# Start of a LoRA and mixture-of-experts kernel: fillers from a constant, raw LoRA products on partition quarters, x in two loads, GpSimd reordered

## The chip, the cores and the metric

The kernel runs on one core of a Trainium2 chip. The metric is the device time of one execution in microseconds (us); lower is better. A core has five engines with a program of their own each: TensorE (PE in the profile; its weight loads are PEld), VectorE (DVE), ScalarE (ACT), GpSimd (POOL) and SyncE (SP), which here only issues DMAs. They wait for each other on semaphores.

## The reference

Input `x` is `[2, 1024, 256]`. Each of its two sequences goes through a ReLU feed-forward layer with LoRA corrections (a common one and one of eight experts, chosen by an input number), and the result through a mixture of experts: a router takes the mean over the tokens, a softmax and the top two of eight experts; their gelu layers are added with the router's weights. `x` is added at the end.

```python
# L0_cond, x: [2, 1024, 256], F = 1024, rank 16 + 16, ALPHA = 2
hidden_i = x @ wi.T + ALPHA * (x @ common_wi_a.T) @ common_wi_b.T + ALPHA * (x @ Wa[e].T) @ Wb[e].T
hidden_i = relu(hidden_i)
hidden_o = hidden_i @ wo.T + (the same two corrections with the wo factors)
# L0_ffn
probs = softmax(hidden_o.mean(axis=1) @ gate_w)
top_w, top_i = top_k(probs, 2);  top_w /= top_w.sum()
out = sum over the two experts e of top_w * (gelu(hidden_o @ w1[e] + b1[e]) @ w2[e] + b2[e])
return x + out
```

## The kernel before

**Tiling.** All data is kept transposed: 256 channels are two halves (`kd` 0 and 1) of 128 partitions, tokens are columns, and a tile is 128 x 512. The hidden width of 1024 is cut into four sets of 256 columns. Two sequences of the first layer and two sequences times two experts of the second make six stages of four sets, 24 sets `q` in all. Sets 0 to 7 belong to the first layer. In each set TensorE makes four hidden tiles ("up"), ScalarE applies ReLU or gelu, and TensorE adds the products of these with the "down" weights to four output banks. The down products of set q-1 lie between the up products of set q.

**Precision.** Each fp32 operand is split into a high part (ScalarE rounds it to fp32r: `up_high`, `down_high`, `x0_high`, `hid_high`) and a low part (the rest, by a subtraction on VectorE or GpSimd: `up_low`, `down_low`, `x0_low`, `hid_low`). A product is three matmuls: high x high, high x low, low x high. Some sets use seven products of sums of operands in place of eight (`seven(q)`), which need more preparation (`weight_sums`, `token_sum`, `raw_low`).

**LoRA.** The corrections are not computed as such: the product of the two factors, 256 x 256 for each set, is added to the weights (`merge_up`, `merge_down` on VectorE, with ALPHA). The factors come in five "lots" of 512 columns for each sequence (`load_lora`); of each, 96 partitions are held as high, high's rest and so on in `lora_st`, so that one fp32r matmul of 96 rows makes all three terms (`up_factor`, `down_factor`). For the sets 0 and 1 of the first sequence this would be too late: `raw_up_factor` multiplies the factors in fp32 as they come, from an own small load, `lora_first` (32 partitions x 768 columns).

**Start.** TensorE waits for a memset of VectorE, runs twelve bf16 fillers of 512 columns (`warm_up`), then the two `raw_up_factor` calls (each two fp32 matmuls of 256 columns over 32 partitions, which the profile shows as four), `first_pair(0)` and `first_pair(1)` (set 0, twelve matmuls for each half of the tokens), and `down_factor(0)`. VectorE merges the first product into set 0's weights in two halves (`merge0`), ScalarE rounds them (`up0_high`), VectorE takes the rests.

**Queues.** Each engine's work is an order written out by hand; nothing is moved at run time. SyncE loads the expert's number, then issues in this order: `lora_first`, x0T of kd 1, x0bT (second half of the tokens, 512 KB), set 1's up weights, LoRA lots 1 and 0, down weights, and so on. ScalarE's queue issues x0T of kd 0 and set 0's up weights. GpSimd makes `up_low` and `down_low` of nearly all sets one set ahead.

Of the kernel before, what the change touches and what calls it, by code (L numbers as in the profile page):

```python
# [13 lines left out]
P = 128  # L14
# [5 lines left out]
def build(nc, ids, x0T, x0bT, x1T, wiT, woT, early, lora, gate, w1, w2, b12, outT):  # L20
# [108 lines left out]
    WARM_UP = 12  # L129

    with ExitStack() as ctx:
# [11 lines left out]
        zeros = y_sb[:, 0, 0:TOK // 2].bitcast(BF16)  # L143
# [9 lines left out]
        lora_first = sb("lora_first", [G, LOT + SW])  # L153
# [30 lines left out]
        s_x0b, s_x1 = sem("s_x0b"), sem("s_x1")  # L184
        s_lora_first = sem("s_lora_first")
# [60 lines left out]


# [58 lines left out]
        def _(eng):  # L306
# [3 lines left out]
            def load_lora(b, lot, e):  # L310
                if b:
                    eng.wait_ge(s_llo[0][lot], 2)
# [9 lines left out]
            def next_down(q):  # L322
# [61 lines left out]
        def _(eng):  # L384
# [55 lines left out]
            def lora_low(b, lot):  # L440

                eng.wait_ge(s_lhi, LORA_HI.index((b, lot)) + 1)
                for n in range(2):
                    lora_lo(eng, b, lot, n)
                    eng.wait_ge(s_llo[b][lot], n + 1)
# [31 lines left out]
            for q in range(1, NSET):  # L477
# [28 lines left out]
                elif q == 5:  # L506
                    logit_terms(0)
                    term_low(0)

# [3 lines left out]
                    token_sum(1, 0)  # L513
                    token_sum(1, 1)
                    down_low(5)
                elif q == 6:
# [4 lines left out]
                    raw_low(eng, 1, 2)  # L521
                    raw_low(eng, 1, 3)
                    down_low(6)
# [25 lines left out]
        def _(eng):  # L549
# [4 lines left out]
            def x0b_high(kd):  # L554
                eng.wait_ge(s_x0b, 16)
                eng.activation(act_hi[:, 0, kd * NT + 1, :], x_sb[:, 0, 1, kd, :], ACT.Copy).then_inc(s_x0hi, 1)

            def lora_high(b, lot):
                eng.wait_ge(s_lora[b][lot], 16)
                if b and lot >= 2:  # L560
                    eng.wait_ge(s_prod, product_count("d", lot - 1))
                eng.activation(lora_st[:, block(0, LOT).start + lot_at(b, lot):lot_at(b, lot) + LOT],
                               lora_raw[0:LR, block(lot, LOT)], ACT.Copy).then_inc(s_lhi, 1)

            def up0_high(kd):
                eng.wait_ge(s_merge0, kd + 1)
                cols = block(kd, SW)
# [110 lines left out]
            x0_high(1)  # L678
            x0b_high(0)
# [79 lines left out]
        def _(eng):  # L759
# [35 lines left out]
            def first_pair(t):  # L795


                for kd in range(KD):
                    eng.wait_ge(s_x0hi, t * KD + kd + 1)
                    eng.wait_ge(s_up0hi, kd + 1)  # L800
                    for f in range(2):
                        w = up_hi[:, 0, block(kd * 2 + f)]
                        eng.matmul(hid_ps[:, 2 * t + f, :], w, act_hi[:, 0, kd * NT + t, :], start=(kd == 0), stop=False)  # L803
                    eng.wait_ge(s_x0lo[kd][t], 1)
                    for f in range(2):
                        w = up_hi[:, 0, block(kd * 2 + f)]
                        eng.matmul(hid_ps[:, 2 * t + f, :], w, act_lo[:, 0, kd * NT + t, :], start=False, stop=False)  # L807
                for f in range(2):
                    for kd in range(KD):
                        eng.wait_ge(s_up0lo, kd + 1)  # L810
                        ins = eng.matmul(hid_ps[:, 2 * t + f, :], up_lo[:, 0, block(kd * 2 + f)],  # L811
                                         act_hi[:, 0, kd * NT + t, :], start=False, stop=(kd == KD - 1))
                    ins.then_inc(s_up, 1)
# [36 lines left out]
            def out_free(q, j):  # L850
                g, t = GROUP_FIRST.index(q), tiles(q)[j][1]
                if g == 0:
                    eng.wait_ge(s_merge0, KD)
# [34 lines left out]
            def raw_up_factor(q, *outs):  # L888

                eng.wait_ge(s_lora_first, 16)  # L890
                own = block(1 + q, SW)
                for kd in range(KD):
                    ins = eng.matmul(outs[kd], lora_first[:, block(kd)], lora_first[:, own], start=True, stop=True)  # L893
                    if q == 0:
                        ins.then_inc(s_prod0, 1)
                if q:
                    ins.then_inc(s_prod, 1)

            def up_factor(q, *outs):
                b, i = seq_of(q), q % SETS  # L900
                for lot in lots_of("u", q):
                    eng.wait_ge(s_llo[b][lot], 2)
# [6 lines left out]
            def down_factor(q, out):  # L909
                b, i = seq_of(q), q % SETS  # L910
                for lot in lots_of("d", q):
                    eng.wait_ge(s_llo[b][lot], 2)
# [48 lines left out]

            def warm_up(count):
                for _ in range(count):
                    eng.matmul(hid_ps[:, 0, :], zeros[:, 0:P], zeros, start=True, stop=True)  # L964
# [54 lines left out]
        def _(eng):  # L1019
            def lora_low(b, lot):  # L1020
                eng.wait_ge(s_lhi, LORA_HI.index((b, lot)) + 1)
                for n in range(2):
                    lora_lo(eng, b, lot, n)

            def merge0(kd):
                if kd == 0:
                    eng.wait_ge(s_up_raw[0], 16)
                eng.wait_ge(s_prod0, kd + 1)
                cols = block(kd, SW)
                eng.scalar_tensor_tensor(out=up_raw[:, 0, cols], in0=out_ps[:, kd, 0:SW], scalar=ALPHA,  # L1030
# [309 lines left out]
```

## Time and profile before

| | |
|---|---|
| median of 3 runs | 267.23 us (266.0 to 267.31) |
| profiled execution | 266.88 us |
| its span, first to last instruction | 265.1 us |
| mean granted TensorE clock | 1.000 |
| TensorE busy | 260.9 us, 98% |
| TensorE weight loads busy | 212.3 us, 80% |
| VectorE, ScalarE, GpSimd busy | 174.7, 175.3, 165.2 us |
| DMA | 19.76 MB, mean 75 GB/s; 303 GB/s over the first 20 us |

Times in rows are microseconds from the first instruction. An engine that shows as busy nearly all the time sets the time of the kernel; the other engines' idle time costs nothing unless TensorE waits for them. TensorE's matmuls are pipelined: a record of 0.39 us is followed by the next after 0.23 us, so the step from start to start tells the rate, and a longer step a loss.

### The profile page before, as it was taken

To read this page: it belongs to the slowest core of one execution; us is meant where nothing else is said; L and a number is where in the kernel's file an instruction comes from. 1 tells how busy PE (TensorE), PEld (TensorE's weight loads), DVE (VectorE), ACT (ScalarE), POOL (GpSimd) and SP (SyncE) were. 2 spreads that over 40 slices of the span, in tenths; PEclk is the share of its full clock that TensorE was granted. 3 is DMA by queue.
4 is the path that set the end of the run, shared out by engine and by line. 5 is a ranking of instruction groups with operands and counts; after the bars stand their busy time and mean duration, and the time that the engine had idled before them with its cause. 6 is when DMAs were issued, how large, how long until landed. Compare 5 with 4: busy or idle time off the path is not lost.

```text
span 265.1 us, 3631 instructions
## 1 busy us (share of the span) xinstructions
PE 260.9 (98%) x1153; PEld 212.3 (80%) x1153; DVE 174.7 (66%) x287; ACT 175.3 (66%) x280; POOL 165.2 (62%) x199
## 2 busy tenths in 40 slices
PE   8999999999999999999999999999999999999995
PEld 2778888888787878888888888888888888888884
DVE  0783767385997936667595767657866566665665
ACT  2757464558625379988986887676677676775650
POOL 2176998964958978798539999466366366331100
PEclk9999999999999999999999999999999999999999
DMA  5996120201042012202202112202102206000004
GB/s 190 368 351 215 42 79 0 84 1 40 0 122 79 8 73 80 82 6 74 83 0 57 31 74 79 80 0 81 66 16 79 70 12 199 0 0 0 2 1 158
DMA packets 11139, 19.76 MB, mean 75 GB/s; under 512 B 2000, under 2 KB 2256, under 8 KB 10992
## 3 DMA queue, kind: packets, MB, share of 16 engines
q1 hardware_dynamic: 10544, 18.61, 21.9%
q10 hardware_dynamic: 576, 0.92, 1.0%
q8 instruction: 9, 0.15, 0.2%
q14 instruction: 10, 0.08, 0.1%
HBM read 17.43 MB, written 2.10 MB: 74 GB/s over the span
## 4 chain that ended last, share of the span: by engine, by line
PE 98%; DVE 0%; issue 0%
PE out_ps L767 16%; PE out_ps L763 16%; PE out_ps L764 16%; PE hid_ps L763 14%; PE hid_ps L764 14%; PE hid_ps L767 14%; PE hid_ps L964 2%; PE hid_ps L803 1%; PE out_ps L893 1%; PE hid_ps L807 1%; PE hid_ps L811 1%; PE hid_ps L915 1%; PE hid_ps L905 1%; DVE x_sb L1276 0%; DVE y_sb L1164 0%
## 5 line engine op out<-in xcount | busy, mean ns | idle before, releaser
L413 POOL TENSOR_TENSOR up_lo<-up_raw,up_hi 128x512 fp32r<-128x512 f32 x42 | 54.4, 1313 | 37.0 <-ACT up_hi L578 34.0
L767 PE MATMUL out_ps<-hid_hi,down_lo 128*128 128x512 f32 x190 | 74.2, 390 | 0.0
L763 PE MATMUL out_ps<-hid_hi,down_hi 128*128 128x512 f32 x190 | 74.1, 390 | 0.0
L764 PE MATMUL out_ps<-hid_lo,down_hi 128*128 128x512 f32 x190 | 74.0, 389 | 0.0
L763 PE MATMUL hid_ps<-act_hi,up_hi 128*128 128x512 f32 x165 | 64.6, 392 | 0.0
L764 PE MATMUL hid_ps<-act_lo,up_hi 128*128 128x512 f32 x165 | 64.3, 390 | 0.0
L767 PE MATMUL hid_ps<-act_hi,up_lo 128*128 128x512 f32 x165 | 64.2, 389 | 0.0
L610 ACT ACTIVATE hid_ps<-hid_ps,bias_sb 128x512 f32<-128x512 f32 x64 | 42.2, 659 | 28.9 <-DVE hid_ps L1085 17.8
L1059 DVE SCALAR_TENSOR_TENSOR hid_lo<-hid_ps,mix,hid_hi 128x512 fp32r<-128x512 f32 x64 | 47.8, 747 | 20.2 <-ACT hid_hi L624 19.6
L419 POOL TENSOR_TENSOR down_lo<-down_raw,down_hi 128x512 fp32r<-128x512 f32 x24 | 31.9, 1328 | 33.2 <-ACT down_hi L588 33.2
L624 ACT ACTIVATE hid_hi<-hid_ps,mix 128x512 fp32r<-128x512 f32 x64 | 44.1, 689 | 5.0 <-ACT hid_ps L610 0.4
L1085 DVE TENSOR_TENSOR hid_ps<-hid_ps,r_sb 128x512 f32<-128x512 f32 x57 | 38.0, 694 | 8.8 <-PE hid_ps L767 8.7
L767 PEld LDWEIGHTS out_ps<-hid_hi,down_lo 128*128 128x128 f32 x190 | 35.7, 188 | 8.3 <-POOL down_lo L419 0.9
L763 PEld LDWEIGHTS out_ps<-hid_hi,down_hi 128*128 128x128 f32 x190 | 35.7, 188 | 7.3
L764 PEld LDWEIGHTS out_ps<-hid_lo,down_hi 128*128 128x128 f32 x190 | 35.7, 188 | 7.3
L763 PEld LDWEIGHTS hid_ps<-act_hi,up_hi 128*128 128x128 f32 x165 | 31.0, 188 | 6.5 <-issue 0.3
L767 PEld LDWEIGHTS hid_ps<-act_hi,up_lo 128*128 128x128 f32 x165 | 31.0, 188 | 6.6
L764 PEld LDWEIGHTS hid_ps<-act_lo,up_hi 128*128 128x128 f32 x165 | 31.0, 188 | 5.8
L618 ACT ACTIVATE hid_hi<-hid_ps 128x512 fp32r<-128x512 f32 x32 | 18.9, 595 | 24.1 <-PE out_ps L767 16.4
L1059 DVE SCALAR_TENSOR_TENSOR hid_lo<-hid_ps,hid_hi 128x512 fp32r<-128x512 f32 x32 | 21.7, 683 | 10.3 <-ACT hid_hi L618 10.1
L578 ACT ACTIVATE up_hi<-up_raw 128x1024 fp32r<-128x1024 f32 (+1 forms) x23 | 22.5, 979 | 7.3 <-POOL up_raw L405 6.0
L1069 DVE TENSOR_TENSOR r_sb<-hid_ps,r_sb 128x512 f32<-128x512 f32 x19 | 13.1, 690 | 17.2 <-PE hid_ps L767 13.6
(98 smaller groups left out, 245.1 us busy)
## 6 DMA issues: line engine op xcount, KB each, us to landing
up_raw<-in_w SPq DMA_DIRECT2D x16, 256.0 KB, 2.8
down_raw<-in_w SPq DMA_DIRECT2D x16, 256.0 KB, 2.7
lora_raw<-in_lora SPq DMA_DIRECT2D x10, 256.0 KB, 4.3
down_raw<-in_woT SPq DMA_DIRECT2D x8, 256.0 KB, 3.4
up_raw<-in_wiT SPq DMA_DIRECT2D x7, 256.0 KB, 4.3
outT<-x_sb SPq DMA_DIRECT2D x6, 256.0 KB, 3.5
x_sb<-in_x1T SPq DMA_DIRECT2D x1, 1024.0 KB, 7.9
x_sb<-in_x0bT SPq DMA_DIRECT2D x1, 512.0 KB, 3.8
```

Of the source, the lines that this page charges most:

```text
L413: ins = eng.tensor_tensor(up_lo[:, n, cols], up_raw[:, n, cols], f32(up_hi[:, n, cols]), ALU.subtract)
L419: eng.tensor_tensor(down_lo[:, n, :], down_raw[:, n, :], f32(down_hi[:, n, :]), ALU.subtract)\
L578: eng.activation(up_hi[:, n, 0:up_width(q)], up_raw[:, n, 0:up_width(q)], ACT.Copy).then_inc(s_up_hi, 1)
L610: eng.activation(hid_ps[:, j, :], hid_ps[:, j, :], ACT.Gelu, bias=bias_sb[:, b, k, f:f + 1])\
L618: eng.activation(hid_hi[:, j, :], hid_ps[:, j, :], ACT.Relu).then_inc(s_hid_hi, 1)
L624: eng.activation(hid_hi[:, j, :], hid_ps[:, j, :], ACT.Copy, scale=mix[:, b, k:k + 1])\
L763: eng.matmul(out, w_h, a_h, start=start, stop=False, skip_group_check=onto)
L764: eng.matmul(out, w_h, a_l, start=False, stop=False, skip_group_check=onto)
L767: return eng.matmul(out, w_l, a_h, start=False, stop=stop, skip_group_check=onto)
L1059: eng.scalar_tensor_tensor(out=hid_lo[:, j, :], in0=hid_ps[:, j, :], scalar=scalar, in1=f32(hid_hi[:, j, :]), op0=op, op1=ALU.subtract).th ...
L1069: eng.tensor_tensor(r2_sb[:, :], hid_ps[:, 1, :], r1_sb[:, :], ALU.add).then_inc(s_r2, 1)
L1085: eng.tensor_tensor(hid_ps[:, j, :], hid_ps[:, bank, :], addend[:, :], ALU.add).then_inc(s_add, 1)
```

## The change

- The fillers multiply a built-in constant of ones (a tensor that is set before the program's body) in place of a part of `y_sb` that VectorE clears first; ten in place of twelve, with an eleventh between the two raw products.
- The loads for the raw products are two: `first_rows`, 128 partitions x 256 columns (128 KB), and `second_rows`, 64 x 384 (96 KB). The first product is four fp32 matmuls of 128 columns, each on 32 partitions of its own (a quarter) and into a bank of its own; the second is two of 256 columns on two quarters.
- Set 0's merge is in three parts (128, 128 and 256 columns), and so is its rounding; `first_half` asks for the parts in another order than `first_pair` did. `second_half` takes the low part of x last.
- x's second half of the tokens is loaded in two DMAs of 256 KB, each with a semaphore of its own.
- Of lots (0, 0) and (0, 2) only the half that is read later is rounded and subtracted (`parts`).
- VectorE's order at the start: `merge_up(1)` after both `x0_low` of the second half, `hid_low(0, 0)` ahead of `lora_low(0, 1)`.
- GpSimd: in set 5 `token_sum(1, 0)` goes ahead of the wait for the router's maximum; in set 6 `down_low(6)` ahead of `raw_low(1, 3)`.
- SyncE reads the first expert's number without bounds.

```diff
-    WARM_UP = 12
+    WARM_UP = 10
...
-        zeros = y_sb[:, 0, 0:TOK // 2].bitcast(BF16)
...
-        lora_first = sb("lora_first", [G, LOT + SW])
+        first_rows = sb("first_rows", [P, 2 * P])
+        second_rows = sb("second_rows", [2 * G, P + SW])
...
+        def parts(b, lot):
+
+            return {(0, 0): [0], (0, 2): [1]}.get((b, lot), [0, 1])
...
+        FIRST_COLS = [slice(0, P), slice(P, SW), slice(SW, 2 * SW)]
+
+        def first_product(n):
+
+            return hid_ps[:, 2 + n, :] if n < 2 else out_ps[:, n - 2, :]
...
-            e = number(ids[0:1, 0:1])
-            eng.dma_start(lora_first[:, :], early[bass.ds(e, 1), :, :].rearrange("e r c -> (e r) c"))\
-               .then_inc(s_lora_first, 16)
+
+            e = eng.value_load(ids[0:1, 0:1])
+            eng.dma_start(first_rows[:, :], first[bass.ds(e, 1), :, :].rearrange("e r c -> (e r) c"))\
+               .then_inc(s_first_rows, 16)
+            eng.dma_start(second_rows[:, :], second[bass.ds(e, 1), :, :].rearrange("e r c -> (e r) c"))\
+               .then_inc(s_second_rows, 16)
             load_x0(eng, 1)
-            eng.dma_start(x_sb[:, 0, 1, :, :], x0bT[:, :, :]).then_inc(s_x0b, 16)
+            for kd in range(KD):
+                eng.dma_start(x_sb[:, 0, 1, kd, :], x0bT[kd, :, :]).then_inc(s_x0b[kd], 16)
...
                     term_low(0)
+                    token_sum(1, 0)
 
 
                     eng.wait_ge(s_nmax, 1)
                     up_low(6)
-                    token_sum(1, 0)
                     token_sum(1, 1)
                     down_low(5)
...
                     raw_low(eng, 1, 2)
+                    down_low(6)
                     raw_low(eng, 1, 3)
-                    down_low(6)
...
+            def first_half():
+
+                eng.wait_ge(s_x0hi, 1)
+                for f in range(2):
+                    eng.wait_ge(s_up0hi, f + 1)
+                    first_one(0, f, 0, False, False, start=True)
+                    if f == 0:
+                        eng.wait_ge(s_x0lo[0][0], 1)
+                    first_one(0, f, 0, False, True)
+                eng.wait_ge(s_up0lo, 1)
+                for f in range(2):
+                    first_one(0, f, 0, True, False)
+                eng.wait_ge(s_x0hi, 2)
+                eng.wait_ge(s_up0hi, 3)
+                for f in range(2):
+                    first_one(0, f, 1, False, False)
+                eng.wait_ge(s_x0lo[1][0], 1)
+                for f in range(2):
+                    first_one(0, f, 1, False, True)
+                eng.wait_ge(s_up0lo, 2)
+                for f in range(2):
+                    first_one(0, f, 1, True, False, stop=True).then_inc(s_up, 1)
...
+            def first_up_factor():
+
+
+                eng.wait_ge(s_first_rows, 16)
+                for n in range(4):
+                    rows = block(n, G)
+                    ins = eng.matmul(first_product(n)[:, 0:P], first_rows[rows, 0:P], first_rows[rows, P:2 * P],
+                                     start=True, stop=True)
+                ins.then_inc(s_prod0, 1)
+
+            def second_up_factor():
+
+                eng.wait_ge(s_second_rows, 16)
                 for kd in range(KD):
...
+                    rows = block(kd, G)
+                    ins = eng.matmul(out_ps[:, 2 + kd, 0:SW], second_rows[rows, 0:P], second_rows[rows, P:P + SW],
+                                     start=True, stop=True)
+                ins.then_inc(s_prod, 1)
...
-            eng.wait_ge(s_zero, 1)
+                    eng.matmul(hid_ps[:, 0, :], filler[:, 0:P], filler, start=True, stop=True)
+
             warm_up(WARM_UP)
-            raw_up_factor(0, out_ps[:, 0, 0:SW], out_ps[:, 1, 0:SW])
-            raw_up_factor(1, out_ps[:, 2, 0:SW], out_ps[:, 2, SW:2 * SW])
-            first_pair(0)
-            first_pair(1)
+            first_up_factor()
+            warm_up(1)
+            second_up_factor()
+            first_half()
+            eng.wait_ge(s_merge0, len(FIRST_COLS))
+            second_half()
+            eng.wait_ge(s_merge, product_count("u", 1))
             down_factor(0, out_ps[:, 3, :])
...
             merge0(0)
             merge0(1)
+            merge0(2)
             up0_low(0)
+            x0_low(eng, 1, 0)
             up0_low(1)
-            x0_low(eng, 1, 0)
             x0_low(eng, 0, 1)
-            merge_up(1, out_ps[:, 2, :])
             x0_low(eng, 1, 1)
+            merge_up(1, out_ps[:, 2:4, 0:SW])
+            hid_low(0, 0)
             lora_low(0, 1)
-            hid_low(0, 0)
             hid_low(0, 1)
```

## Rows read from the trace of the kernel before

**Rows 1.** Busy time, share of the span and instructions of each engine.

```profile
PE 260.9 (98%) x1153; PEld 212.3 (80%) x1153; DVE 174.7 (66%) x287; ACT 175.3 (66%) x280; POOL 165.2 (62%) x199
```

**Rows 2.** Waits of TensorE's weight loads: us in total, times, longest us.

```profile
PEld out_ps L767 <- POOL down_lo L419: 0.9, 3, 0.5
...
PEld hid_ps L905 <- issue: 0.4, 1, 0.4
```

**Rows 3.** Chain that ended last, in time: start us, us, what.

```profile
10.35 0.93 PE hid_ps L811 x4
```

**Rows 4.** Timeline of the start: start us, us, engine, line, operation [idle before].

```profile
0.74 0.33 POOL L386 MEMSET rank<- 128x1 f32 x8 [0.29 <-POOLq L1330]
...
1.20 5.16 PE L964 MATMUL hid_ps<-y_sb 128*128 128x512 bf16 x12 [1.20 <-DVE y_sb L1164]
...
2.92 0.40 SPq L328 DMA_DIRECT2D lora_first<-in_early  x1
...
3.37 0.48 SPq L264 DMA_DIRECT2D x_sb<-in_x0T  x1
...
4.99 0.89 SPq L314 DMA_DIRECT2D lora_raw<-in_lora  x2
```

**Rows 5.** Timeline of TensorE, single matmuls from the last filler on.

```profile
5.87 0.49 PE L964 MATMUL hid_ps<-y_sb 128*128 128x512 bf16 x1
...
6.28 0.48 PE L893 MATMUL out_ps<-lora_first 32*128 32x256 f32 x1
...
6.60 0.38 PE L893 MATMUL out_ps<-lora_first 32*128 32x256 f32 x1
...
7.90 0.37 PE L893 MATMUL out_ps<-lora_first 32*128 32x256 f32 x1
...
8.20 0.50 PE L803 MATMUL hid_ps<-act_hi,up_hi 128*128 128x512 f32 x1
```

**Rows 6.** Timeline of VectorE and ScalarE at set 0's merge.

```profile
7.10 0.77 DVE L1030 SCALAR_TENSOR_TENSOR up_raw<-out_ps,up_raw 128x256 f32<-128x256 f32 x2 [5.70 <-PE out_ps L893]
7.55 0.77 ACT L568 ACTIVATE up_hi<-up_raw 128x256 fp32r<-128x256 f32 x2 [3.40 <-DVE up_raw L1030]
```

**Rows 7.** DMA issues in short stretches: KB each, us from issue to landing.

```profile
lora_first<-in_early SPq DMA_DIRECT2D x1, 96.0 KB, 2.1
...
x_sb<-in_x0T SPq DMA_DIRECT2D x1, 256.0 KB, 3.0
...
lora_raw<-in_lora SPq DMA_DIRECT2D x1, 256.0 KB, 5.0
```

**Rows 8.** Timeline from 10 to 19 us, what feeds the sets 1 and 2.

```profile
10.09 0.68 DVE L1043 SCALAR_TENSOR_TENSOR up_raw<-out_ps,up_raw 128x512 f32<-128x512 f32 x1
...
12.56 1.46 POOL L413 TENSOR_TENSOR up_lo<-up_raw,up_hi 128x512 fp32r<-128x512 f32 x1 [7.07 <-ACT up_hi L578]
...
14.31 0.19 PEld L767 LDWEIGHTS hid_ps<-act_hi,up_lo 128*128 128x128 f32 x1
...
16.26 2.03 DVE L244 TENSOR_TENSOR lora_st<-lora_raw,lora_st 32x256 fp32r<-32x256 f32 x2
```

**Rows 9.** Timeline of GpSimd in set 5.

```profile
66.30 2.56 POOL L413 TENSOR_TENSOR up_lo<-up_raw,up_hi 128x512 fp32r<-128x512 f32 x2 [2.80 <-DVE neg_max L1117]
68.80 2.55 POOL L434 TENSOR_TENSOR t_sum<-y_sb 128x512 f32<-128x512 f32 x2
71.31 1.29 POOL L419 TENSOR_TENSOR down_lo<-down_raw,down_hi 128x512 fp32r<-128x512 f32 x1
```

**Rows 10.** Timeline of TensorE in the sets 5 and 6.

```profile
72.23 0.39 PE L764 MATMUL out_ps<-hid_lo,down_hi 128*128 128x512 f32 x1
72.66 0.50 PE L767 MATMUL out_ps<-hid_hi,down_lo 128*128 128x512 f32 x1
...
83.31 0.50 PE L767 MATMUL out_ps<-hid_hi,down_lo 128*128 128x512 f32 x1
83.65 0.39 PE L763 MATMUL out_ps<-hid_hi,down_hi 128*128 128x512 f32 x1
```

More of the change, by code:

```diff
@@ L17, with build @@
 TOP_K = 2
-def build(nc, ids, x0T, x0bT, x1T, wiT, woT, early, lora, gate, w1, w2, b12, outT):
+def build(nc, ids, x0T, x0bT, x1T, wiT, woT, first, second, lora, gate, w1, w2, b12, outT):
     D, NTOK = outT.shape
@@ L311, in load_lora @@
                 if b:
-                    eng.wait_ge(s_llo[0][lot], 2)
+                    eng.wait_ge(s_llo[0][lot], len(parts(0, lot)))
                 cols = block(lot, LOT)
@@ L442, in lora_low @@
                 eng.wait_ge(s_lhi, LORA_HI.index((b, lot)) + 1)
-                for n in range(2):
+                for made, n in enumerate(parts(b, lot)):
                     lora_lo(eng, b, lot, n)
-                    eng.wait_ge(s_llo[b][lot], n + 1)
+                    eng.wait_ge(s_llo[b][lot], made + 1)
             def logit_terms(b):
@@ L554, in x0b_high @@
             def x0b_high(kd):
-                eng.wait_ge(s_x0b, 16)
+                eng.wait_ge(s_x0b[kd], 16)
                 eng.activation(act_hi[:, 0, kd * NT + 1, :], x_sb[:, 0, 1, kd, :], ACT.Copy).then_inc(s_x0hi, 1)
             def lora_high(b, lot):
+                made = parts(b, lot)
+                to = slice(lot_at(b, lot) + made[0] * SW, lot_at(b, lot) + (made[-1] + 1) * SW)
+                raw = slice(lot * LOT + made[0] * SW, lot * LOT + (made[-1] + 1) * SW)
                 eng.wait_ge(s_lora[b][lot], 16)
@@ L561, in lora_high, with up0_high @@
                     eng.wait_ge(s_prod, product_count("d", lot - 1))
[L562 to L567, printed above, removed]
+                eng.activation(lora_st[:, to], lora_raw[0:LR, raw], ACT.Copy).then_inc(s_lhi, 1)
+            def up0_high(n):
+                eng.wait_ge(s_merge0, n + 1)
+                cols = FIRST_COLS[n]
                 eng.activation(up_hi[:, 0, cols], up_raw[:, 0, cols], ACT.Copy).then_inc(s_up0hi, 1)
@@ L678, in _ @@
             x0_high(1)
+            up0_high(2)
             x0b_high(0)
@@ L793, in first_low, with first_one @@
                 return up_lo_made(q)
-            def first_pair(t):
+            def first_one(t, f, kd, low_w, low_a, start=False, stop=False):
+                w, a = (up_lo if low_w else up_hi), (act_lo if low_a else act_hi)
+                return eng.matmul(hid_ps[:, 2 * t + f, :], w[:, 0, block(kd * 2 + f)], a[:, 0, kd * NT + t, :],
+                                  start=start, stop=stop)
+            def first_half():
[19 more added lines that the diff above has]
+                    first_one(0, f, 1, True, False, stop=True).then_inc(s_up, 1)
@@ L805, in first_pair @@
                     for f in range(2):
[L806 to L813, printed above, removed]
+                        first_one(1, f, kd, True, False)
@@ L815, in plain_tile @@
+                for kd in range(KD):
+                    eng.wait_ge(s_x0lo[kd][1], 1)
+                    for f in range(2):
+                        ins = first_one(1, f, kd, False, True, stop=(kd == KD - 1))
+                        if kd == KD - 1:
+                            ins.then_inc(s_up, 1)
             def plain_tile(q, j):
@@ L901, in up_factor @@
                 for lot in lots_of("u", q):
-                    eng.wait_ge(s_llo[b][lot], 2)
+                    eng.wait_ge(s_llo[b][lot], len(parts(b, lot)))
                 for kd in range(KD):
@@ L911, in down_factor @@
                 for lot in lots_of("d", q):
-                    eng.wait_ge(s_llo[b][lot], 2)
+                    eng.wait_ge(s_llo[b][lot], len(parts(b, lot)))
                 for f in range(2):
@@ L1321 @@
         "woT": down_sets(t(a["L0_cond_wo"])),
-        "early": np.concatenate([up_a, up_b[:, :, 0:2 * SW]], axis=2)[:, 0:up_a.shape[1] // 4],
+        "first": up_rows(0, P),
+        "second": up_rows(1, SW),
         "lora": np.concatenate(lots, axis=2),
```

60 lines of the change are left out of this document (30 added, 30 removed).

## The prediction, made before the changed kernel was run

> **What bounds the kernel now.** I read the busy table first: TensorE works 260.9 of 265.1 us [rows 1], so a change pays only where it removes time in which TensorE stands, or work that TensorE does before the real products. The waits come second, and there only those of TensorE and its weight loads are worth looking for: weight loads waited three times, 0.9 us together, for a `down_lo` of GpSimd, and once 0.4 us ahead of a LoRA factor (`L905`) [rows 2]. A weight load may wait while an earlier matmul still streams, so the true loss is less; the steps between matmuls tell it, below. Then the start, instruction by instruction [rows 4, 5]: TensorE runs its first filler at 1.20, when VectorE's memset is done, and works without a pause from there, but until 8.20 it does nothing of the result except the four raw LoRA matmuls. From 8.20 the bound is the count of matmuls times the step of 0.23 us (four in 0.93) [rows 3]. So the question is when the matmul at 8.20 can start after the change, and whether what feeds TensorE until about 19 us keeps up with the earlier start.
>
> **The clock at the start.** The granted clock reads 1.00 throughout, but it isn't what the first fillers show: twelve take 5.16 us including the last one's end, 0.427 us from one to the next, which for 512 columns is the 1.2 GHz level [rows 4]. The steps of `L893` from 6.60 to 7.90 are 0.217 us for 256 columns in fp32 (six steps; each fp32 matmul shows as two passes, so eight records for four), the same rate per column as the 512-column step of 0.23 further on, which is the 2.4 GHz level [rows 3, 5]. The level had changed by 6.60, and hardly before 6.0, as the step from the twelfth filler at 5.87 to the first LoRA pass is still 0.41 [rows 5]. I take 6.1 us, and keep it at that place for the changed kernel, since TensorE is busy from 0.35 us earlier but by no more.
>
> **1. The fillers.** They no longer wait for a memset. The other engines' first instructions are at 0.74 [rows 4]; I take 0.8 for the first filler, 0.4 earlier than 1.20. Two fillers fewer are 2 x 0.427 = 0.85. The first LoRA matmul could then start at 6.28 - 0.40 - 0.85 = 5.03. Its operand, 128 KB in place of 96 KB, is issued on SyncE's queue where `lora_first` was, at 2.92, and that one landed 2.1 us later, at 5.0 [rows 4, 7]. So the two meet; 0 to 0.3 us of waiting is the bound (32 KB more, four times as many rows of a third of the length, against a bounds test less on SyncE). Sum: the LoRA products start at 5.05, 1.23 earlier.
>
> **2. The first product.** It is four fp32 matmuls of 128 columns (eight passes), each on its own quarter of the partitions, in place of two of 256. At the high level a pass is half of 0.217, 0.11; at the low level 0.22. No row of before shows quarters side by side. The upper bound is none: eight passes, 4.8 of them before 6.1 and the rest at 0.11, done at 6.45. The lower bound is four quarters at once: two passes of 0.22, done at 5.5. I take a value between: the second pass of one matmul goes with the first of the next, as they use different quarters, so five passes of 0.22, done at 6.1; the order of issue allows this and no row forbids it. *What the Trainium skill says:* "TensorE: Matmul & The Clock Gate", in "Packing small matmuls", gives 3.07x for four quarter matmuls of K=32 and 512 columns. By that figure, as an estimate, the eight passes would be done 0.4 to 0.5 us sooner than I take; no row of before shows it.
>
> The merge into `up_raw` started at 7.10, 0.50 after the last pass that it needed (6.60) [rows 5, 6]. With the last of my five steps starting at 5.9 it starts at 6.4. It works on 128 columns: 256 took 0.425 (a pair in 0.77) and 512 take 0.68 [rows 6, 8], so 128 take 0.30. ScalarE's rounding of these columns takes 0.31 by the same slope, where a pair of 256 took 0.77 and the first followed the merge by 0.45 [rows 6]. 6.4 + 0.30 + 0.31 and 0.12 of handing over: the first real matmul has its weights at 7.13.
>
> **3. What TensorE does in that time.** A thirteenth filler at the high level (0.22) and the second product, two fp32 matmuls of 256 columns on two quarters: four passes of 0.217 = 0.87, or three steps = 0.65 if neighbours overlap as above. Going between 128-row and 32-row matmuls costs something: 7.90 to 8.20 is 0.30 where a pass is 0.217, and 5.87 to 6.28 is about 0.1 more than its columns need [rows 5]. So 0.1 at each change, of which the filler between the products adds two. 6.1 + 0.1 + 0.22 + 0.1 + 0.65 + 0.1 = 7.27, later than 7.13, so TensorE's own queue sets it: first real matmul at 7.27, 0.93 before 8.20. The bounds: without overlap 6.45 + 0.1 + 0.22 + 0.1 + 0.87 + 0.1 = 7.84, a gain of 0.36; all quarters at once, about 6.65, a gain of 1.55. *The Trainium skill* states in "TensorEngine Tiling (Array Packing)", "Key Properties", that changing the tiling mode drains TensorE. It speaks against the filler in the middle. The trace agrees as far as 0.1 us a change; a full drain of the 0.37 us that an `L893` record lasts would put the sum 0.5 us later.
>
> **4. Keeping up until the second set.** The new order in `first_half` asks for `up_lo` and x's second half of the depth sooner. VectorE's list from 6.4: three merges (0.30, 0.30, 0.43) to 7.45, `up_lo` of kd 0 to 7.9, `act_lo` of kd 1 (0.68) to 8.6, `up_lo` of kd 1 to 9.05. TensorE at 0.23 a step from 7.27 wants them at 8.2, 9.1 and 9.6. These are hidden, with 0.3 to 0.5 us to spare. x0T of kd 1 landed at 3.37 + 3.0 = 6.4 and is now one DMA issue (0.45) later, 6.85; it is rounded about 7.4, so it is hidden too; when it is more than 0.8 late, TensorE stands for the rest. Splitting `x0bT` adds an issue, not bytes.
>
> Every later load on SyncE moves by two issues, 0.9 us, at most; by bytes (128 KB more, where the queue brought x's second half, set 1 and a lot, 1 MB, from 6.4 to 10.0, 284 KB a us) by 0.45 [rows 4, 7]. I take 0.45. The load of LoRA lot 1 then lands at 10.45 in place of 4.99 + 5.0. ScalarE rounds it to 11.1, then set 1's weights to 11.75 (behind `merge_up`, which VectorE now does last of its start list, 10.4 to 11.1); VectorE, after `hid_low(0, 0)`, makes the lot's low parts to 12.65; GpSimd the low half of set 1 in 1.46 to 13.2. TensorE reaches `down_factor(0)` at 7.27 + 24 x 0.23 = 12.7 and the low half 0.7 later, 13.4. In before GpSimd was done at 14.02 and the weights were taken at 14.31 [rows 8]. So it stays covered, by 0.05 and 0.2: nothing now, but 0.2 to 0.4 us lost if the loads come the full 0.9 later. That is the price for the new order of `merge_up` and `hid_low`.
>
> **5. Parts of lots.** Lots (0, 0) and (0, 2) lose the low part that nobody reads: GpSimd saves two of its four 32x256 subtractions, some 0.7 us each. VectorE's pair for lot 3 took 2.03 us from 16.26 to 18.29 while GpSimd did the same kind, and `L905` behind it waited [rows 2, 8]. That wait was 0.4; a weight load of 0.19 can be hidden under the matmul before it, so about 0.2 is lost. With GpSimd less busy I take half, 0.1; bounds 0 and 0.23.
>
> **6. GpSimd reordered.** In set 5 it stood 2.80 us for the router's maximum. Moving `token_sum(1, 0)`, half of a pair of 2.55, ahead of that wait lies wholly in the gap, and `down_low(5)` comes 1.28 sooner [rows 9]. TensorE lost 0.43 - 0.23 = 0.20 in front of 72.66 and 0.11 in that record (0.50, not 0.39), 0.31; it needed `down_lo` 0.2 sooner, so all of it goes [rows 10]. In set 6 `down_low(6)` goes ahead of one `raw_low`: the step from 83.31 to 83.65 is 0.34, so 0.11 back. The moved `raw_low(1, 3)` is late by one subtraction, but its reader is set 8, many us later. Together 0.42; bounds 0.2 and 0.45.
>
> **Sum.** 0.93 + 0.1 + 0.42 = 1.45 us, all on TensorE's path and never given back, since the rest is TensorE step by step. The profiled execution took 266.88 us with a span of 265.1, which is 0.35 below the median of the runs, 267.23. So 265.4 for an execution like the profiled one, 265.8 from the median; I say 265.6.
>
> **The rivals.** *(a) Quarters don't overlap.* The first real matmul at 7.84: gain 0.36 + 0.52 = 0.9, 266.2, no measurable change. For it: all records of before on one quarter step in file. *(b) Quarters all at once*, two passes of 0.22: gain 1.55 + 0.52 = 2.1, 265.0. Against it: the passes of one matmul share a quarter, and the merge chain then binds at about 6.6. *(c) Loads late.* Five DMAs where three were ahead of set 1 cost the full 0.9 us and TensorE stands at `down_factor(0)` or `up_lo`; gain 1.45 - 0.5 = 0.95, 266.2, same. *(d) The clock stays low longer, the slower side.* If the pause for `first_rows` and the quarter products put the rise off, each us of real work at the low level costs 0.5. The gain is gone when it comes 2.9 us later than 6.1, at 9.0, and the kernel is slower by over 0.5% from 11.8 us on: 268.7 then. For it: ten fillers, not twelve, stand ahead, and the level rose only in the twelfth; against it, TensorE has work nearly throughout. *(e) The early matmul is absorbed*: the end is set elsewhere, so nothing changes, 267.2. The busy table speaks against it.
>
> **How the numbers follow.** My forecast 0.42, its own range 265.2 to 266.0; (a) 0.18, (b) 0.15, (c) 0.12, (d) 0.07 (of it half slower than the bound), (e) and others 0.06. The range reaches from (b), 264.6 with the luck of the clock's rise, to 267.0, which leaves out (e) and most of (d). A measurement here tells about 0.5%, 1.3 us, from nothing; that bound, 265.9, lies close above my number, so faster gets 0.54: two thirds of my forecast and nearly all of (b), and parts of (a) and (c) when the clock rises early. Slower gets 0.06.
>
> **What would show it.** In the profile after: fillers from about 0.8; the first product at 5.0 to 5.1 with steps between passes of different quarters below those of one; the first merge near 6.4; the first real matmul near 7.3; `down_factor(0)` near 12.7 (12.3 to 13.2); the step before the factor near 17.5 below 0.43; no wait for `down_lo` in sets 5 and 6, so that the fillers' start and the count of real matmuls alone explain a span near 263.6. The prediction is wrong when 0.217-us steps run in file through the quarters, when weight loads wait between 12 and 15 us, or when matmuls of 512 columns are 0.43 apart after 7.3.

## The result and the profile after

The changed kernel takes 267.63 us in the median of 19 runs (266.17 to 269.06); the kernel before, run 19 times beside it, 266.60. The ratio is 1.0033, with a 95% interval of 1.002 to 1.0045: about 0.9 us slower, where 1.6 us less was forecast and 267.0 was the upper end of the range. The profiled execution has a span of 265.8 us (267.63 in all), 0.7 more than the one of before. Ratios and their intervals here are worked out from the single executions, so they are not the quotients of the two medians. They leave out three slow executions that the medians keep: 534.2 us in the kernel before with the set 6 order, 269.21 and 269.34 us with all products on one quarter.

The busy table of the changed kernel, the line that answers to [rows 1]:

```profile
PE 259.0 (97%) x1156; PEld 211.3 (79%) x1156; DVE 176.3 (66%) x288; ACT 175.1 (66%) x281; POOL 164.0 (62%) x197
```

TensorE works 1.9 us less and the span is 0.7 longer, so it stands 2.6 us more. Its waits (us in total, times, longest us) say for whom; the same view of before has one line, the wait of 1.2 for the memset:

```profile
PE out_ps L965 <- DVE lora_st L245: 1.6, 1, 1.6
...
PE hid_ps L782 <- DVE act_lo L295: 0.6, 1, 0.6
PE hid_ps L936 <- DMA first_rows<-in_first: 0.6, 1, 0.6
```

Three places. The start first, in the timeline of the changed kernel; the lines answer to [rows 4 to 6]:

```profile
0.78 3.64 PE L1016 MATMUL hid_ps<-const-bfloat16-1.0 128*128 128x512 bf16 x10 [0.78 <-PEq L1400]
...
4.99 0.38 PE L936 MATMUL hid_ps<-first_rows 32*128 32x128 f32 x2 [0.56 <-DMA first_rows<-in_first]
5.00 0.38 PE L936 MATMUL out_ps<-first_rows 32*128 32x128 f32 x2
...
5.42 0.39 PE L1016 MATMUL hid_ps<-const-bfloat16-1.0 128*128 128x512 bf16 x1
...
5.64 0.49 DVE L1087 SCALAR_TENSOR_TENSOR up_raw<-hid_ps,up_raw 128x128 f32<-128x128 f32 x2 [4.38 <-PE out_ps L936]
...
5.97 0.70 PE L945 MATMUL out_ps<-second_rows 32*128 32x256 f32 x4 [0.16 <-DMA second_rows<-in_second]
...
6.60 0.50 PE L816 MATMUL hid_ps<-act_hi,up_hi 128*128 128x512 f32 x1
```

This part went better than forecast: the eight passes of the first product lie within 0.43 us (4.99 to 5.42), the first merge is at 5.64 and the first real matmul at 6.60, where 6.4 and 7.27 were forecast and 8.20 was the value of before. The second product starts at 5.97, when `second_rows` has landed, a wait of 0.16 us that the prediction did not price. The gain of 1.60 us is lost on the way to `down_factor(0)`, here the timeline from 10 to 14 us:

```profile
10.07 0.69 DVE L283 TENSOR_TENSOR act_lo<-x_sb,act_hi 128x512 fp32r<-128x512 f32 x1 [0.88 <-ACT act_hi L572]
...
10.68 0.63 ACT L581 ACTIVATE lora_st<-lora_raw 96x512 fp32r<-96x512 f32 x1
...
11.28 0.68 DVE L1120 SCALAR_TENSOR_TENSOR hid_lo<-hid_ps,hid_hi 128x512 fp32r<-128x512 f32 x1
...
11.99 1.82 DVE L245 TENSOR_TENSOR lora_st<-lora_raw,lora_st 32x256 fp32r<-32x256 f32 x2
12.11 1.43 POOL L429 TENSOR_TENSOR up_lo<-up_raw,up_hi 128x512 fp32r<-128x512 f32 x1 [6.54 <-ACT up_hi L596]
```

Single records of the same stretch:

```profile
12.44 1.37 DVE L245 TENSOR_TENSOR lora_st<-lora_raw,lora_st 32x256 fp32r<-32x256 f32 x1
...
11.97 0.39 PE L816 MATMUL hid_ps<-act_lo,up_hi 128*128 128x512 f32 x1
13.96 0.36 PE L965 MATMUL out_ps<-lora_st 96*128 96x256 f32 x1 [1.60 <-DVE lora_st L245]
```

TensorE issues its last matmul of set 0 at 11.97 and the LoRA factor only at 13.96. It waits for VectorE's two subtractions on LoRA lot (0, 1). The second, 32 partitions x 256, takes 1.37 us: it was issued at 12.44, while GpSimd's `up_low(1)` ran from 12.11 to 13.54, and ended at 13.81, after it. In the kernel before the pair was at 11.99 too and its second subtraction at 12.44 as well, but GpSimd came at 12.56 [rows 8], 0.12 us behind the start of both, and the pair took 0.86 us:

```profile
11.99 0.86 DVE L244 TENSOR_TENSOR lora_st<-lora_raw,lora_st 32x256 fp32r<-32x256 f32 x2 [0.63 <-ACT lora_st L562]
```

The same holds in all twelve profiled executions of this case. VectorE issues such a 32x256 subtraction 26 times while a GpSimd operation with two inputs runs; each ends 0.28 us after GpSimd's. The other 22 take 0.41 or 0.42 us.

The third place is sets 6 to 8. GpSimd's timeline, VectorE's last `sum_low` of set 7, and TensorE at set 8, in the changed kernel:

```profile
79.03 1.29 POOL L289 TENSOR_TENSOR act_lo<-y_sb,act_hi 128x512 fp32r<-128x512 f32 x1
81.27 1.30 POOL L435 TENSOR_TENSOR down_lo<-down_raw,down_hi 128x512 fp32r<-128x512 f32 x1 [0.95 <-ACT down_hi L606]
82.53 1.29 POOL L289 TENSOR_TENSOR act_lo<-y_sb,act_hi 128x512 fp32r<-128x512 f32 x1
...
87.69 2.99 POOL L429 TENSOR_TENSOR up_lo<-up_raw,up_hi 128x512 fp32r<-128x512 f32 x2 [1.17 <-ACT up_hi L596]
...
91.16 1.78 DVE L295 TENSOR_TENSOR act_lo<-t_sum,act_hi 128x512 fp32r<-128x512 f32 x1
...
92.23 0.39 PE L786 MATMUL out_ps<-hid_hi,down_lo 128*128 128x512 f32 x1
93.20 0.47 PE L782 MATMUL hid_ps<-act_hi,up_hi 128*128 128x512 f32 x1 [0.58 <-DVE act_lo L295]
```

And the lines of the kernel before that answer to them:

```profile
79.44 2.56 POOL L277 TENSOR_TENSOR act_lo<-y_sb,act_hi 128x512 fp32r<-128x512 f32 x2
81.97 1.29 POOL L419 TENSOR_TENSOR down_lo<-down_raw,down_hi 128x512 fp32r<-128x512 f32 x1
...
86.80 2.68 POOL L413 TENSOR_TENSOR up_lo<-up_raw,up_hi 128x512 fp32r<-128x512 f32 x2 [1.17 <-ACT up_hi L578]
...
91.66 0.95 DVE L283 TENSOR_TENSOR act_lo<-t_sum,act_hi 128x512 fp32r<-128x512 f32 x1
...
92.56 0.39 PE L767 MATMUL out_ps<-hid_hi,down_lo 128*128 128x512 f32 x1
92.86 0.47 PE L763 MATMUL hid_ps<-act_hi,up_hi 128*128 128x512 f32 x1
```

With `down_low(6)` ahead of the second `raw_low`, GpSimd stands 0.95 us for ScalarE's `down_hi`. Before, that time was filled by the second `raw_low`. From there its work is later: the second `raw_low` ends 0.56 us later, and `up_low(8)`, which waits for ScalarE's rounding of the sums that GpSimd makes in between, comes 0.9 us later. So GpSimd's work falls on VectorE's last subtraction for set 8, which takes 1.78 us in place of 0.95. TensorE, 0.33 us ahead of before at 92.23, starts set 8 0.34 us behind it at 93.20.

### The profile page after: what moved, and what is told of

Read it like the earlier page. It is cut to its first block, busy times and chain, and to the rows that moved or that the text cites. A ratio compares the mean times of both kernels' runs of the same rounds, so it can differ in the third digit from the quotient of the medians.

```text
span 265.8 us, 3639 instructions
## 1 busy us (share of the span) xinstructions
PE 259.0 (97%) x1156; PEld 211.3 (79%) x1156; DVE 176.3 (66%) x288; ACT 175.1 (66%) x281; POOL 164.0 (62%) x197
## 4 chain that ended last, share of the span: by engine, by line
PE 91%; DVE 3%; DMA 2%; SPq 1%; issue 1%; ACT 1%; ACTq 0%
PE out_ps L782 16%; PE out_ps L786 16%; PE out_ps L783 16%; PE hid_ps L782 14%; PE hid_ps L786 14%; PE hid_ps L783 14%; DMA x_sb<-in_x0bT 2%; DVE act_lo L295 1%; DVE lora_st L245 1%; DVE act_lo L289 1%; PE hid_ps L955 1%; SPq L340 1%; PE hid_ps L965 1%; DVE hid_lo L1120 0%; DVE up_raw L1104 0%
```

## The experiments

The times in this section are medians of the kernel and, beside it on the same chip, of the kernel before.

**One swap on VectorE.** Only the order at the start:

```diff
             merge_up(1, out_ps[:, 2:4, 0:SW])
-            hid_low(0, 0)
             lora_low(0, 1)
+            hid_low(0, 0)
```

> The changed kernel with one pair of VectorE's list swapped back: the low parts of LoRA lot (0, 1) ahead of hid_low(0, 0). Theory A (VectorE's subtraction cannot start while GpSimd works on up_low(1), and takes 1.37 us instead of 0.42): the subtractions run at about 11.4 to 12.2, ahead of GpSimd's start at 12.1, take 0.42 each, TensorE's pause of 1.99 us ahead of down_factor(0) shrinks to under 0.5, and set 1 starts about 1.2 us sooner (13.0 instead of 14.27); 1.0 to 1.3 us less in all than the changed kernel. Rival B (the later landing of the lot, 10.7 instead of 10.0, is the cause): the pause shrinks by 0.3 us at most. The stalls of 0.74 and 0.35 us at sets 8 and 9 stay in both.

266.48 beside 266.37 us, ratio 1.0004 (0.9988 to 1.002). Timeline of this kernel:

```profile
11.37 0.86 DVE L245 TENSOR_TENSOR lora_st<-lora_raw,lora_st 32x256 fp32r<-32x256 f32 x2 [0.22 <-ACT lora_st L581]
...
11.94 1.45 POOL L429 TENSOR_TENSOR up_lo<-up_raw,up_hi 128x512 fp32r<-128x512 f32 x1 [6.49 <-ACT up_hi L596]
...
12.27 1.29 DVE L1120 SCALAR_TENSOR_TENSOR hid_lo<-hid_ps,hid_hi 128x512 fp32r<-128x512 f32 x2
...
12.38 0.47 PE L965 MATMUL out_ps<-lora_st 96*128 96x256 f32 x2
...
13.10 0.47 PE L782 MATMUL hid_ps<-act_hi,up_hi 128*128 128x512 f32 x1 [0.25 <-DVE hid_lo L1120]
```

ScalarE rounds the lot no earlier than in the changed kernel (10.71 there, 10.68 in the latter), so the later load of the lot isn't the cause of the long subtraction. The subtractions take 0.43 us each again, and set 1 starts at 13.10 in place of 14.27, 1.17 sooner, as theory A gave. The span is 264.7, 1.1 less; the ratio is 0.0029 lower, 0.8 us. And `hid_low`, which has one input in PSUM, runs its two in 1.29 us right under GpSimd's record: it isn't held up. (Its kind, 128x512, starts under such a GpSimd operation 724 times in the twelve traces, and none takes over 0.75 us.)

**One swap on GpSimd.**

```diff
                     raw_low(eng, 1, 2)
-                    down_low(6)
                     raw_low(eng, 1, 3)
+                    down_low(6)
```

> The changed kernel with GpSimd's order in set 6 put back: both raw_low, then down_low(6). Theory A (GpSimd stood 0.95 us for ScalarE's down_hi with work behind it, so that its later work fell on VectorE's sum_low in set 7): the steps of 0.97 and 0.58 us ahead of sets 8 and 9 return to 0.30, the 0.34 step at about 83 us comes back (0.11), in all 0.8 to 0.9 us less than the changed kernel. Rival B (those stalls come from the start's other shifts): they stay, and the time gets longer by 0.1 us.

266.54 beside 266.37 us, ratio 1.0006 (0.9987 to 1.0025), span 264.7. TensorE's matmuls ahead of set 8:

```profile
92.12 0.39 PE L786 MATMUL out_ps<-hid_hi,down_lo 128*128 128x512 f32 x1
92.44 0.47 PE L782 MATMUL hid_ps<-act_hi,up_hi 128*128 128x512 f32 x1
```

The step is 0.32, where the changed kernel has 0.97. Both raw_low are in one group of 2.56 us from 78.91 and `down_low(6)` follows without a wait. The expected step of 0.34 at set 6 did not come back: with set 5's gain, `down_low(6)` is in time anyhow, so the swap had nothing left to give there.

**Both swaps.**

> Both swaps together. If the two losses are independent and are all that ate the gain, the time is the changed kernel's less 2.0 us: 0.9 us or so below the kernel before (ratio about 0.996). Rival: something else in the start (clock, loads) costs too, and it only ties with the kernel before.

265.80 beside 266.37 us, ratio 0.9982 (0.9967 to 0.9996), span 263.5. In ratios the swaps give 0.0029 and 0.0027 alone and 0.0051 together, so they are two losses, not one. The time is 1.4 us below the changed kernel's by ratio, less than the 2.0 expected; the spans differ by 2.3.

**GpSimd waits.** This was meant to separate the collision from everything else that is late: VectorE keeps the changed order, and GpSimd does `after((s_llo[0][1], 2))` ahead of `up_low(1)`.

> The changed kernel, VectorE's order as changed, but GpSimd waits with up_low(1) until VectorE has made both low parts of lot (0, 1). Theory A (the two engines exclude each other in such subtractions): VectorE's second subtraction takes 0.42 us again, down_factor(0) starts at about 12.95 instead of 13.96, though GpSimd is done only at 14.2, so set 1's third matmul waits for it; a gain of 0.3 to 0.5 us. Rival B (lateness of the load alone, or a slow subtraction for its own reasons such as the operands' place): the subtraction still takes 1.37 us, and the time is longer by 1 us as GpSimd is later too.

266.95 beside 266.37 us, ratio 1.0026 (1.0011 to 1.0042), span 264.8. Its timeline:

```profile
11.61 0.86 DVE L245 TENSOR_TENSOR lora_st<-lora_raw,lora_st 32x256 fp32r<-32x256 f32 x2
...
12.55 1.28 POOL L429 TENSOR_TENSOR up_lo<-up_raw,up_hi 128x512 fp32r<-128x512 f32 x1 [7.08 <-DVE lora_st L245]
...
12.62 0.48 PE L966 MATMUL out_ps<-lora_st 96*128 96x256 f32 x2
...
13.89 0.49 PE L787 MATMUL hid_ps<-act_hi,up_lo 128*128 128x512 f32 x1 [0.33 <-POOL up_lo L429]
```

The pair takes 0.86 us, although the lot was rounded at 10.88, later than in the changed kernel. But this execution alone doesn't separate the causes: x's second half of the tokens could be rounded from 9.02 here and from 9.41 in the changed kernel, the pair began 0.38 us sooner (11.61, not 11.99), and its second subtraction, at 12.06, would just have been ahead of a GpSimd that starts at 12.11 as in the changed kernel. The collision is shown by the pair in the traces of before and after, where the second subtraction starts at 12.44 in both and GpSimd's start differs, by the first swap, and by the 26 records above. The factor comes 1.3 us sooner, but then set 1's third matmul waits for `up_lo`, issued late, as expected. The span gains 1.0, the ratio 0.0007 only, which the intervals don't tell from nothing.

**The kernel before with one of the two GpSimd edits.**

> The kernel before, with only GpSimd's order in set 6 as in the change (down_low(6) ahead of the second raw_low). Theory A (GpSimd then stands about 0.95 us for ScalarE's down_hi, and what follows falls on VectorE's sum_low in set 7): the steps ahead of sets 8 and 9 grow from 0.30 to 0.7 to 1.0 and 0.5 to 0.6 us, and the kernel is 0.7 to 0.9 us slower, ratio 1.003. Rival (the loss needs the changed start): no difference, or 0.1 us faster. Its start is that of the kernel before, so its fillers also show when the clock rises in another execution: the first real matmul comes at 7.4 to 9.0, earlier than 8.20 when the rise is earlier than in the execution shown.

268.02 beside 266.82 us, ratio 1.005 (1.0034 to 1.0066), nine executions, one of them the 534.2 us that nothing here explains: the set 6 order alone costs 1.3 us, more than expected. TensorE's matmuls ahead of set 8:

```profile
91.84 0.39 PE L767 MATMUL out_ps<-hid_hi,down_lo 128*128 128x512 f32 x1
93.60 0.47 PE L763 MATMUL hid_ps<-act_hi,up_hi 128*128 128x512 f32 x1 [1.37 <-DVE act_lo L283]
```

A step of 1.76 us. Here GpSimd and VectorE get in each other's way twice more ahead of it (GpSimd's second raw_low takes 1.82 us, not 1.29). So the loss needs nothing of the changed start.

> The kernel before, with only token_sum(1, 0) ahead of the wait for the router's maximum in set 5. By the steps of TensorE in the kernel before, 0.31 us come back at 72.7 us and nothing else moves; ratio 0.999. Rival (as in set 6, an earlier piece of GpSimd's work falls on VectorE and slows it): the router's chain gets longer, no gain. The start is that of the kernel before and gives one more execution to read the clock from.

265.80 beside 266.82 us, ratio 0.9972 (0.9955 to 0.9988), span 264.0. The long steps at sets 5 and 6 (0.43, 0.34 and 0.34 for 0.23) are gone, 0.42 us; the one at set 6 too, which the prediction had given to the set 6 order. The measured 0.75 us (0.3 to 1.2) holds that. And this execution, whose start is the unchanged one, shows what the shown execution of before hid:

```profile
3.73 2.04 PE L964 MATMUL hid_ps<-y_sb 128*128 128x512 bf16 x6
5.71 1.99 PE L893 MATMUL out_ps<-lora_first 32*128 32x256 f32 x8
7.63 0.50 PE L803 MATMUL hid_ps<-act_hi,up_hi 128*128 128x512 f32 x1
```

The same twelve fillers end 0.57 us sooner than in [rows 5], since the clock rose sooner, and the first real matmul is at 7.63 instead of 8.20; in the other one (the set 6 order alone) it is at 7.61.

**The fillers alone, in the kernel before.**

```diff
-    WARM_UP = 12
+    WARM_UP = 10
...
-                    eng.matmul(hid_ps[:, 0, :], zeros[:, 0:P], zeros, start=True, stop=True)
-
-            eng.wait_ge(s_zero, 1)
+                    eng.matmul(hid_ps[:, 0, :], filler[:, 0:P], filler, start=True, stop=True)
+
```

> The kernel before, with only the fillers changed: from the constant, without the wait, ten. The LoRA products start at 5.0 to 5.1, when lora_first has landed, and the first real matmul 1.9 later, at 6.95, if the level is high by then, and up to 1 us later if not. Theory A (the start of TensorE sets everything as long as VectorE's order is that of the kernel before): 0.5 us faster in the median, ratio 0.998; more against an execution with a late rise, little against one with an early rise, in which twelve fillers end near 5.5 anyway. Rival B (the fillers' gain is lost at down_factor(0), as in the changed kernel): the factor starts no earlier than 13.0 and a pause of over 0.5 us stands ahead of it; ratio 1.000.

266.12 beside 266.82 us, but ratio 1.0007 (0.9977 to 1.0036): no verdict. Seven of twelve executions take 265.7 to 266.2 us, the other five 267.5 to 269.45. The profiled one is of the short kind (span 264.0):

```profile
5.16 1.99 PE L893 MATMUL out_ps<-lora_first 32*128 32x256 f32 x8 [0.19 <-DMA lora_first<-in_early]
7.08 0.50 PE L803 MATMUL hid_ps<-act_hi,up_hi 128*128 128x512 f32 x1
...
12.75 0.40 PE L915 MATMUL out_ps<-lora_st 96*128 96x256 f32 x2
```

No pause stands ahead of the factor at 12.75 (a step of 0.23 us), so in this execution theory A's mechanism holds: with VectorE's old order an early start is kept. In the ratio the long executions eat it.

**All four products on one quarter.**

```diff
-                    rows = block(n, G)
-                    ins = eng.matmul(first_product(n)[:, 0:P], first_rows[rows, 0:P], first_rows[rows, P:2 * P],
-                                     start=True, stop=True)
+                    ins = eng.matmul(first_product(n)[:, 0:P], first_rows[:, block(2 * n)],
+                                     first_rows[:, block(2 * n + 1)], start=True, stop=True)
...
```

> The changed kernel with both swaps back, and the four matmuls of the first product all on one quarter of the partitions (32 rows of 4 KB in place of 128 of 1 KB, the same bytes). If the quarters run side by side, as the steps of 0.01 to 0.1 us in the changed kernel say, in file the eight passes take 8 x 0.11 = 0.9 us at the high level instead of 0.43, the first merge starts 0.4 to 0.5 us later, the first real matmul about 0.3 to 0.5 later, and the time is 0.3 us longer than with both swaps alone. Rival (the gain of the start comes from halving the columns and the earlier fillers, and the later wait for hid_low hides the rest): no difference in time.

266.11 beside 266.82 us, ratio 0.9984 (0.9957 to 1.0012), span 264.2.

```profile
5.01 0.71 PE L935 MATMUL hid_ps<-first_rows 32*128 32x128 f32 x4
5.56 0.60 PE L935 MATMUL out_ps<-first_rows 32*128 32x128 f32 x4
6.10 0.39 PE L1015 MATMUL hid_ps<-const-bfloat16-1.0 128*128 128x512 bf16 x1
...
7.06 0.48 PE L816 MATMUL hid_ps<-act_hi,up_hi 128*128 128x512 f32 x1
```

On one quarter the eight passes take 1.09 us from the first to the next filler, on four 0.43 in the changed kernel; in both executions the level was high by then, as the last filler's record of 0.38 us for 0.63 earlier shows. The first real matmul is at 7.06, with the quarters between 6.47 and 6.79 in the kernels with ten fillers and both swaps: 0.3 to 0.6 later. The time doesn't resolve it; again five of twelve executions are long.

**Ten or twelve fillers.**

> The changed kernel with both swaps back and twelve fillers in place of ten ahead of the first product. The executions so far show a mean granted clock of 0.994 in some executions of kernels with ten fillers (3 of 12 of the kernel before with ten, 2 of 12 with one quarter, 1 of 12 or 19 of three others) and times 1.5 to 3.6 us above their median, and never in 67 executions of the kernel before. Theory (TensorE's pause between the tenth filler and the landing of the LoRA rows puts the clock off in these): with twelve no execution reads 0.994 and none is more than 1.5 us above the median; the median is within 0.4 us of the one with ten, as the fillers end at 5.0 to 5.9, about when the rows land. Rival (the level's timing is chance and has nothing to do with the count): as many long executions as with ten, and the median longer by 0.4 to 0.8 us for the two fillers.

265.46 beside 266.71 us, ratio 0.9962 (0.9949 to 0.9976), 265.3 to 266.2, all of twelve within 0.8 us of the median. No execution is long, as the theory gave; but the next run has none with ten either, so the two don't tell theory from rival.

> The changed kernel with both swaps back, a second time, beside the one with twelve fillers on the same chip. If its first ratio of 0.998 was no accident, again 0.995 to 0.999; long executions in about one of twelve if ten fillers cause them.

265.41 beside 266.71 us, ratio 0.9949 (0.993 to 0.9967), eight executions, none long. TensorE at the start, first with twelve, then with ten:

```profile
0.78 4.64 PE L1016 MATMUL hid_ps<-const-bfloat16-1.0 128*128 128x512 bf16 x12 [0.78 <-PEq L1400]
...
6.79 0.47 PE L816 MATMUL hid_ps<-act_hi,up_hi 128*128 128x512 f32 x1
```

```profile
0.78 3.99 PE L1016 MATMUL hid_ps<-const-bfloat16-1.0 128*128 128x512 bf16 x10 [0.78 <-PEq L1400]
...
6.47 0.50 PE L816 MATMUL hid_ps<-act_hi,up_hi 128*128 128x512 f32 x1
```

Either is faster than the kernel before, here by 0.4 to 0.5%, in the first run of the one with ten by 0.2%; and, by ratio, faster than the changed kernel. What the two fillers cost is not shown: the first real matmul is at 6.79 with twelve and at 6.47 with ten, but it was at 6.79 in the first run with ten too, where the clock rose later.

## Why the prediction was wrong

- **The bound** was read rightly: TensorE sets the time, and each of its pauses came out in the span. The span grew 0.7: -1.60 at the first real matmul, +1.72 from there to the factor (13.96, where it was 13.84), nearly all in the step of 1.99 ahead of it where 0.23 is usual, and at set 8 again +0.67 (0.34 behind after 0.33 ahead) and another 0.4 by set 9 (0.72 behind), against which stand the 0.4 us of sets 5 and 6.
- **Steps 1 to 3, the start**, held in mechanism: 0.78 for the first filler, 4.99 for the product. The size was off in two ways. The quarters ran all at once, which was rival (b), so 6.60 and not 7.27. That (b)'s 6.65 fits so well is in part luck: it counted two passes of 0.22 at the low level, and the level was high by then. In the changed kernel's fillers the step falls from 0.43 to 0.22 at about 3.6 us, not at the 6.1 that I kept, and two rounds on four quarters still took 0.43. The Trainium skill's page "TensorE: Matmul & The Clock Gate", in "Packing small matmuls", had that right in kind: it gives 3.07x for four of 512 columns, and the runs show 1.09 us on one quarter over 0.43 on four, 2.5x. And the comparison was with an execution whose clock rose late: two more executions of the same start have the first real matmul at 7.6, so of the 1.6 us only 1.0 is there against those two, and the runs shown, median 267.23, stood 0.6 above the 266.60 of more runs.
- **Step 4, keeping up, is the step that failed.** It has VectorE make the lot's low parts to 12.65 and calls the new order's price "nothing now, but 0.2 to 0.4 us lost if the loads come the full 0.9 later". They were done at 13.81, and TensorE was there at 12.2: 1.7 us. The loads, which I priced as the danger (rival (c)), came 0.7 later for the lot, where I had 0.45, and the second part of `x0bT` landed at 9.4, where all of it had landed at 7.7. TensorE did not wait for them: with the loads as late, the first swap has the factor at 12.38. But VectorE stood 0.88 us for the rounding of that part, ahead of `merge_up(1)`, so the loads have a share in where its pair fell; how large a share over many executions isn't shown, and the other half of VectorE's new order, `merge_up(1)` behind both `x0_low`, was not put back by itself. What I left out is that a VectorE subtraction with both inputs in SBUF, issued while GpSimd works on one, stands until GpSimd's is done. The trace of before had it in a row that I used: the pair of 2.03 us at 16.26 [rows 8], which I put down to GpSimd being busy with the same kind and took to be a cost of the place, without asking which other pair the shifts would bring under GpSimd. *The Trainium skill* says it in "SBUF — State Buffer", "Who interferes with whom": a VectorE instruction with two SBUF inputs contends with a GpSimd instruction that reads SBUF, and whoever issues first has the shared ports for its whole instruction. The runs agree: 1.37 us behind GpSimd, 0.42 ahead of it, and `hid_low`, with an input in PSUM, unhindered. Put to step 4, by my own times GpSimd starts at 11.75 and VectorE's pair at 11.8. If only the second of the pair is held, it ends 0.28 behind GpSimd's 13.2, at about 13.5; if the first is, the pair ends at about 13.9. That is a stall of 0.8 to 1.2 us at 12.7, and a gain of 0.3 to 0.6 in all. (24 x 0.23 from 7.27 is 12.8, not the 12.7 that I wrote.)
- **Step 5**, half of 0.2 us back at `L905`: wrong, but small. The step there is 0.43 in both kernels, and VectorE's pair ahead of it, from 16.46 now, still runs behind GpSimd's work (1.15 and 0.84 us for 0.42 each).
- **Step 6** is half right. Set 5 gave what was forecast, 0.31, and the 0.11 of set 6 with it. In set 6, "The moved `raw_low(1, 3)` is late by one subtraction, but its reader is set 8, many us later" failed. What was late wasn't that subtraction but all of GpSimd's work behind the new wait of 0.95 us, and that landed on VectorE's subtractions for set 8. I named no queue behind the moved instruction and didn't check when ScalarE's `down_hi` would be ready. It costs 0.0027 of the time in the changed kernel and 0.005 in the kernel before.
- **The rivals.** The slower side was given to the clock alone (d). Executions with a lower clock reading do exist, see below, but the median doesn't come from them. The two mechanisms that decided were none of my rivals.

## What to carry to other kernels

Ahead of moving a VectorE subtraction or a GpSimd one, write down for each pair with two SBUF inputs which of the two engines starts first; the loser waits out the whole other instruction, and a small shift upstream turns the order over: in the kernel before it held by 0.12 us. Moving an instruction up an in-order engine is free only when its own input is ready there: else the engine stands, and the price is paid by everything behind it. And a gain at the start should be counted against several executions' starts, not one, when the level of TensorE's clock changes there.

## What the runs showed that I had not expected

**The clock in some executions with ten fillers.** The mean granted clock of an execution reads 0.999 or 1.000 in 86 executions of the kernel before with known clock, none above 267.43 us. With ten fillers it reads 0.994 in one execution of 19 of the changed kernel (269.06 us), in one of 12 of the second swap alone (268.02) and of the waiting GpSimd (267.87), in none of 12 of the first swap alone, in three of 12 of the kernel before with ten (267.50 to 267.87) and two of 12 on one quarter (267.04, 267.14). These are 0.9 to 1.8 us above the medians of their kernels. The kernel before with ten fillers has two more at 269.4, the one with one quarter three at 269.0 to 269.3, of which the clock reading says nothing (1.000). With both swaps and ten fillers 20 executions had none at 0.994, with twelve 12 had none. TensorE stands between the tenth filler and the landing of the rows (0.56 us in the changed kernel); that this pause is the cause is argued, not shown, since 20 executions without one are too few against rates of 1 in 12. The profiled pauses rather speak against it: 0.64 us in the first swap, with none of 12, and 0.19 in the kernel before with ten, with three of 12. A rival was not tested: the two kernels with the most such executions, five of their 24, ran on one chip, and in the rest it was three of 75. What the long ones with a reading of 1.000 are, stays open.

**Quarters.** Eight fp32 passes of 128 columns on four quarters took 0.43 us, four starting within 0.02 us of each other, and 1.09 us on one.

**A fast swap is small in the code.** The better kernel here, with both swaps back, differs from the changed kernel by the order of two pairs of calls, and is, by ratio, 0.5% or more below it.
